# A two-layer sequence kernel: dt of each scan half made in a new order, deferred products over 60 of 64 steps

## The reference, cut to what matters

```python
xz = einsum('bsd,ed->bse', xn, in_proj_w); x_in, z = split(xz, 2, axis=-1)     # 1024 channels each
u = silu(causal_conv4(x_in) + conv_b)
dt_r, B, C = split(u @ x_proj_w.T, [64, 80], axis=-1)                          # 64, 16, 16 columns
dt = softplus(dt_r @ dt_proj_w.T + dt_proj_b);  A = -exp(A_log)                # A: 1024 x 16
h = h * exp(dt * A) + (dt * u) * B;  y = sum over the 16 states of h * C       # a scan over 1024 positions
y = (y + u * D) * silu(z);  x = x + gate * (y @ out_proj_w.T)
```

## Time and profile before

| | before |
|---|---|
| median of 3 runs (lowest, highest) | 7325.14 us (7324.45, 7329.71) |
| the profiled execution: time, span | 7318.66 us, 7317.1 us |
| PE busy | 6329.8 us (87%) |
| DVE busy | 5947.7 us (81%) |
| ACT busy | 4700.3 us (64%) |
| POOL busy | 3147.3 us (43%) |
| mean granted TensorE clock | 0.93 of 2.4 GHz |

### The profile page before, as it was taken

One profiled execution on the slowest core, in us unless ns is written; L12 is line 12 of the kernel. 1 busy time (PEld: TensorE's weight loads), 2 busy tenths in 40 slices (PEclk: granted clock), 3 DMA queues, 4 the chain that ended last, 5 costly groups with the idle time before them and its releaser, 6 DMA issues.

```text
span 7317.1 us, 135980 instructions
## 1 busy us (share of the span) xinstructions
PE 6329.8 (87%) x43360; PEld 4061.0 (55%) x43360; DVE 5947.7 (81%) x7137; ACT 4700.3 (64%) x6673; POOL 3147.3 (43%) x1533
## 2 busy tenths in 40 slices
PE   6998799987989879989799888898799987999878
PEld 2664457644575546745467445664457644575544
DVE  0678988789887998869978799778988799887995
ACT  2665677566675666746767467665677566675664
POOL 0105771067601774019730388105771067601773
PEclk9999899998999989999899998999899998999989
DMA  3425783367823777238752387425783367823676
GB/s 143 142 76 163 180 202 108 104 161 169 235 59 132 162 173 202 71 129 183 181 164 82 133 204 182 128 75 164 179 203 107 106 161 169 234 59 132 163 173 176
DMA packets 432975, 1092.28 MB, mean 149 GB/s; under 512 B 50056, under 2 KB 50184, under 8 KB 428000
## 3 DMA queue, kind: packets, MB, share of 16 engines
q1 hardware_dynamic: 256672, 671.49, 28.0%
q0 software_dynamic: 157120, 378.04, 26.6%
q10 hardware_dynamic: 18432, 33.56, 1.3%
HBM read 564.39 MB, written 250.10 MB: 111 GB/s over the span
## 4 chain that ended last, share of the span: by engine, by line
PE 70%; issue 10%; DVE 8%; DMA 4%; ACT 3%; POOL 3%; DVEq 1%; SPq 1%; ACTq 0%; POOLq 0%
PE ps L1233 43%; PE ps L1486 11%; PE ps L1334 9%; PE ps L1283 3%; POOL area_s L675 3%; DMA z_keep<-z_st 2%; DVE area_h L1156 2%; DVE area_s L1041 1%; PE ps L1285 1%; ACT k_stack L778 1%; DVE area_dt L1144 1%; PE ps L1435 1%; DMA k_stack<-qk_keep 1%; DMA area_acc<-area_w 1%; DVE area_u L1050 1%
## 5 line engine op out<-in xcount | busy, mean ns | idle before, releaser
L675 POOL TENSOR_TENSOR area_s<-area_u,area_s 128x1024 f32<-128x1024 f32 x1024 | 2537.0, 2547 | 667.3 <-DVE area_u L1147 385.0
L1156 DVE TENSOR_TENSOR_SCAN area_h<-ps,area_s 128x1024 f32<-128x1024 f32 x1024 | 2333.9, 2279 | 32.8 <-POOL area_s L675 19.1
L1486 PEld LDWEIGHTS ps<-ident,area_h 128*128 128x128 f32 x8192 | 1009.8, 151 | 960.8 <-DVE area_acc L1166 480.2
L1486 PE MATMUL ps<-ident,area_h 128*128 128x128 f32 x8192 | 1201.9, 294 | 383.3 <-DVE area_h L1156 205.7
L802 ACT ACTIVATE area_s<-area_s,negmax 128x1024 f32<-128x1024 f32 x1024 | 1177.3, 1150 | 519.8 <-DVE negmax L1041 517.4
L1041 DVE CUSTOM_DVE_ANT_0 area_s<-ps,area_dt 128x1024 f32<-128x1024 f32 x1024 | 1241.5, 1215 | 169.5 <-PE ps L1233 118.3
L662 POOL TENSOR_TENSOR area_s<-area_s 128x1024 f32<-128x1024 f32 x64 | 176.3, 2754 | 2651.8 <-ACT area_s L847 2651.8
L874 ACT ACTIVATE ps<-area_dt,negA 128x1024 f32<-128x1024 f32 x1024 | 1145.9, 1120 | 236.7 <-DVE area_h L1156 119.7
L860 ACT ACTIVATE area_w<-ps,C_nat 128x512 f32<-128x512 f32 x1024 | 704.4, 688 | 827.7 <-PE ps L1486 814.1
L1334 PE MATMUL ps<-ident,area_s 128*128 128x128 f32 x8192 | 1091.0, 277 | 16.6 <-ACT area_s L802 16.6
L1334 PEld LDWEIGHTS ps<-ident,area_s 128*128 128x128 f32 x8192 | 973.1, 143 | 168.7 <-issue 24.7
(11 more groups left out here) (125 smaller groups left out, 5598.8 us busy)
## 6 DMA issues: line engine op xcount, KB each, us to landing
area_acc<-area_w POOLq DMA_DIRECT2D x256, 1024.0 KB, 8.7
area_s<-b_rows SPq DMA_DIRECT2D x256, 512.0 KB, 5.1
q_stack<-qk_keep SPq DMA_DIRECT2D x520, 128.0 KB, 2.6
k_stack<-qk_keep SPq DMA_DIRECT2D x520, 128.0 KB, 3.2
qk_keep<-q_stack SPq DMA_DIRECT2D x144, 256.0 KB, 4.7
qk_keep<-k_stack SPq DMA_DIRECT2D x144, 256.0 KB, 5.2
area_s<-z_keep SPq DMA_DIRECT2D x72, 512.0 KB, 4.4
y_keep<-area_acc POOLq DMA_DIRECT2D x8, 4096.0 KB, 14.6
```

Of the source, the lines that this page charges most:

```text
L675: pool.tensor_tensor(dbu[:, dl % 2, :], U[:, k // (NS * DL) * DL + dl, :], bb[:, q, :], ALU.mult).then_inc(s_dbu.sem, 1)
L1156: v.tensor_tensor_scan(out=hs[:, q, dl, :], data0=banks(2 * (dl % 2)), data1=dbu[:, dl % 2, :], initial=0.0, op0=ALU.mult, op1=ALU.add).th ...
L1486: last = nc.tensor.transpose(ps[:, 4 + n % 2, dl * P:(dl + 1) * P], hs[:, r % 2, dl, n * P:(n + 1) * P], ident[:, :])
```

## The change

Line numbers here and in the rows that follow are those of the kernel before, where not said otherwise; in the listings of the changed order they are the changed kernel's.

- **Banks.** The dt products of tiles 0 to 3 go to banks 0, 2, 6 and 4 (`DT_BANK`), no more to 0, 2, 4, 6.
- **Order of dt.** On DVE clips, the pairs of L1144 and L1147, and scans alternate tile by tile; on ScalarE Exp and Ln of a tile follow one another (`soft`). At the second half PE makes the product of tile 4 behind the third scan of the last state, tile 5 ahead of that state's transposes, tile 6 within them and tile 7 after them, and DVE's and ScalarE's work on them stands between the last state's adds and scalings.
- **One table set.** Ahead of the copy of x_dbl ScalarE loads the set `natural_log_exp_and_others`, which has both functions.
- **Deferred products.** The 128 products are spread over the first 60 steps: product m stands in step m * 60 // 128. A row's flips stand behind its second and fourth `out` product.
- **Output adds** of GpSimd move with the units' steps: to steps 22, 37 and 52 from 23, 39 and 55.

```diff
+DT_BANK = (0, 2, 6, 4)
...
-ROW = 8
-FLIP_LAG, MOVE_LAG = 6, 6
+PRODUCTS, OVER, MOVE_LAG = 16 * NT, 60, 6
+def deferred_at(m):
+    return m * OVER // PRODUCTS
...
-        units.append(("z", j, 0, 7 - p, ROW * j + 1))
+        units.append(("z", j, 0, 7 - p, deferred_at(m + 3)))
...
-            units.append(("flip", j + 1, 0, 6 + p, ROW * j + 4))
-            units.append(("flip", j + 1, 1, 6 + p, ROW * j + 6))
-        units.append(("out", j, 0, 7 - p, ROW * j + 7))
+            units.append(("flip", j + 1, 0, 6 + p, deferred_at(m + 9)))
+            units.append(("flip", j + 1, 1, 6 + p, deferred_at(m + 11)))
+        units.append(("out", j, 0, 7 - p, deferred_at(m + 15)))
...
+                nc.scalar.preload_act_table_set("natural_log_exp_and_others")
                 act.wait_ge(*s_xd.at(b, 1))
...
+                soft(0)
+                soft(1)
+                decay_tile(0, 0, 0)
+                soft(2)
...
+                scale_by_c(0, NS - 2, NT - 1, 0)
+                for i in moves_at(NS * DL, NS * DL + 12):
+                    move_unit(i)
+                soft(4)
+                scale_by_c(0, NS - 1, 1, 1)
+                soft(5)
...
-                    clip(dg * DL + 2)
-                    clip(dg * DL + 3)
...
+                dt_and_dtu(0)
+                clip(2)
+                dt_and_dtu(1)
+                clip(3)
+                scan(0, 0, 0, 0)
...
-                    if s == 4 and j + 1 < NT:
-                        flip(j + 1, 0)
+                    if j + 1 < NT and k in (1, 3):
+                        flip(j + 1, k // 2)
...
+                        if r == NS - 1:
+                            pe.wait_ge(*s_h.at(b, r * DL + 3))
+                            project_dt(DL)
                         pe.wait_ge(*s_h.at(b, (r + 1) * DL))
+                        if r == NS - 1:
+                            project_dt(DL + 1)
...
-                            if r == NS - 1 and step in (1, 2):
-                                project_dt(DL + (step == 2))
+                            if r == NS - 1 and n == 3:
+                                pe.wait_ge(*s_ge.at(b, NU))
+                                project_dt(DL + 2)
+                        if r == NS - 1:
+                            pe.wait_ge(*s_acc.at(b, NS * DL))
+                            pe.wait_ge(*s_ev.at(b, NS * DL))
+                            project_dt(DL + 3)
```

More of the change, by code:

```diff
@@ new lines, in _ @@
+                soft(0)
+                soft(1)
+                decay_tile(0, 0, 0)
+                soft(2)
+                decay_tile(0, 0, 1)
+                soft(3)
+                decay_tile(0, 0, 2)
+                decay_tile(0, 0, 3)
+                for r in range(1, NS):
+                    decay(0, r)
+                scale_by_c(0, NS - 2, NT - 1, 0)
+                for i in moves_at(NS * DL, NS * DL + 12):
+                    move_unit(i)
+                soft(4)
+                scale_by_c(0, NS - 1, 1, 1)
@@ new lines, in _ @@
+                soft(5)
+                scale_by_c(0, NS - 1, 3, 1)
+                decay_tile(1, 0, 0)
+                scale_by_c(0, NS - 1, 5, 1)
+                scale_by_c(0, NS - 1, 7, 1)
+                decay_tile(1, 0, 1)
+                soft(6)
+                decay_tile(1, 0, 2)
+                soft(7)
+                decay_tile(1, 0, 3)
+                act.wait_ge(*s_zs.at(b, 16 * ZU))
+                act.nop(nofuse=True)
+                for r in range(1, NS):
+                    decay(1, r)
@@ L941, in _ @@
+                scale_by_c(1, NS - 2, NT - 1, 0)
+                for n in range(1, NT, 2):
+                    scale_by_c(1, NS - 1, n, 1)
+                    for _, i, low in copies_at(NS * DL + n // 2, NS * DL + 12 if n == NT - 1 else None):
+                        copy_unit(b + 1, i, low)
             for s in range(NT + 1):
@@ new lines, in _ @@
+                dt_and_dtu(0)
[3 more added lines that the diff above has]
+                scan(0, 0, 0, 0)
+                dt_and_dtu(2)
+                scan(0, 0, 0, 1)
+                dt_and_dtu(3)
+                scan(0, 0, 0, 2)
+                scan(0, 0, 0, 3)
+                with dve.Fori(0, NS // 2 - 1) as i:
+                    for q in (1, 0):
+                        for dl in range(DL):
+                            scan(0, i * 2 + (2 - q), q, dl)
+                            add(0, i * 2 + (1 - q), 2 * dl)
@@ new lines, in _ @@
+                for dl in range(DL):
+                    scan(0, NS - 1, 1, dl)
+                    add(0, NS - 2, 2 * dl)
+                clip(4)
+                clip(5)
+                add(0, NS - 1, 0)
+                add(0, NS - 1, 2)
+                dt_and_dtu(4)
+                add(0, NS - 1, 4)
+                dt_and_dtu(5)
+                add(0, NS - 1, 6)
+                clip(6)
+                scan(1, 0, 0, 0)
+                dt_and_dtu(6)
+                clip(7)
+                scan(1, 0, 0, 1)
@@ L1209, in _ @@
+                dt_and_dtu(7)
+                scan(1, 0, 0, 2)
+                scan(1, 0, 0, 3)
+                dve.wait_ge(*s_dul.at(b, 16))
+                for r in range(1, NS):
+                    for dl in range(DL):
+                        scan(1, r, r % 2, dl)
+                        add(1, r - 1, 2 * dl)
+                        next_norm(r * DL + dl)
+                for n in range(0, NT, 2):
+                    add(1, NS - 1, n)
             dve.wait_ge(*s_acc.at(B - 1, UN))
```

302 lines of the change are left out of this document (125 added, 177 removed).

## The result

The changed kernel takes **7388.58 us** (median; 7378.7 to 7395.76), the kernel before, measured beside it, 7324.8 us: ratio 1.0085, 95% interval 1.0067 to 1.0102. It is slower by 64 us where 18 us less was forecast.

A forecast was written before the change was run, and what follows sets the result against it. The prediction took DVE and PE as level and full in the first half, nothing near full at the seams. Per element -5.3 + 8.0 - 4.9 = -2.2, for eight -18, on the median 7325.1: 7307 us, range 7250 to 7347.

The forecast's parts named there:

- Seam 1: Opening of an element's first half, where dt is made: the new order on DVE gains 5.3 us per element.
- Table loads: ScalarE's table loads, nine fewer and one added per element: worth nothing, since they lie beside DVE's work.
- The second multiply: DVE's second multiply in the first seam: overlaps GpSimd's product by only 0.1 us, taken as 0 extra.
- Seam 2: Opening of the second half: starts right behind GpSimd's output add, then waits for du's load; gains 4.9 us per element.
- the free steps: The first half's last four steps, left without deferred products: DVE alone could begin the new half well before.
- The flips' waits: First half, before flips in even rows: PE waits for ScalarE to empty their PSUM bank, 5.4 us lost per element.
- Rival A: Waits at the flips don't count: the half costs 1 us instead of 8, 7251 us; chance 0.20.
- z's waits: First half: ScalarE's copies into z's one buffer come closer, waits for stores grow, 3.4 us per element landing on PE.
- PE's clock behind a stop: First half: half speed counted only at the opening, 3.0 us as before; nothing added behind PE's waits.
- Half: First half from PE's first step to its last: 178.1 us instead of 170.1, 8.0 us lost per element.
- Rival B: First half: z's late stores make all eight copy pairs wait, 12.2 us instead of 3.4, 7378 us; chance 0.12.

The follow-up runs named there:

- table_only: The kernel before with only the one table set loaded ahead of the copy of x_dbl, all orders as before: 7321.73 us, ratio 0.9998.
- over64: The changed kernel with deferred products over 64 steps again instead of 60, new order of both seams kept: 7253.87 us, ratio 0.9903.
- spread_only: The kernel before with only the deferred products spread over 60 steps, flips, copies and output adds moving along: 7415.84 us, ratio 1.0123.
- z_two: The changed kernel with two buffers for z's copies instead of one: 7286.96 us, ratio 0.9945.
- two_moves_first: The changed kernel with two buffers for z's copies and ScalarE's copies of deferred units ahead of its scaling: 7257.79 us, ratio 0.991.
- moves_first: The changed kernel with ScalarE's copies of deferred units ahead of its scaling in the same step: 7275.27 us, ratio 0.9932.
- parts_step0: The changed kernel with GpSimd's accumulating transfers of the parts issued one step earlier: 7405.4 us, ratio 1.0112.

## Why the prediction was wrong

The forecast was 7307, range 7250 to 7347; measured 7389. The chance of slower was 0.20.

- **Seam 1, 5.3 us per element: right.** First scan 651.12, 7.38 us after the last u·D product instead of 12.6; 7.3 was forecast. Over eight elements it gave 4.3 each, since the first element's old seam (12.63) was the longest; the others had 11.1 to 12.1. Taking one element eight times was 8 us too much.
- **Table loads, 0: right**, shown by table_only.
- **The second multiply, 0 extra: right.** It took 1.26 us, beside GpSimd's product of 646.57 to 648.93. The Trainium skill, "SBUF — State Buffer" (two separate sides), lets only their overlap count, 0.18 us as an estimate; the trace agrees in that the cost is no more than that: 0.03 us above the first multiply's 1.23.
- **Seam 2, 4.9 us: right in size**, 4.8 measured, and in its chain: GpSimd's product behind the output add, du's load last. I had du's 2 MB at 9.1 by its row; DVE's wait ended 10.6 after the issue. The Trainium skill, "DMA: Bandwidth & Descriptors" (Anatomy of one DMA), gave 6.8 as an estimate by its fit for GpSimd's transfers, and a gain of 5.3; the trace does not agree. But I put the gain down partly to the free steps. over64 shows that the order of dt alone gives it, spread_only that the free steps alone would have given it too; they don't add up.
- **The flips' waits, 5.4: right mechanism, measured 4.0** (z_two); the half gave back 2.5 of them when they were taken away (two_moves_first). Rival A is thereby out: PE has no room, its stops do count.
- **z's waits, 3.4: here it fell.** The step was "The two copies of a row are 2 x 2.84 = 5.68 apart now, 5.18 at PE's own pace, so each wait grows by 0.5". It let the copies move and kept the landing. The landing is not a property of the store: 6.7 us behind a part's transfer it is 5.4, 1.75 behind it 8.0 (row 4 in both kernels). The change moved 16 copies per element against transfers that stay on every fourth step, and the forecast never laid the two lists of steps side by side, though it did so for the output adds. The waits are 8.6 us per element (1.9 before), and the two buffers give back 11.9.
- **PE's clock behind a stop, 0: missed.** The sum counted a wait as its length. The opening's half speed stood in the same rows, and the low clock comes back behind a stop: 0.57 granted over 4 us behind row 4's, 1.5 us lost, 15 such stretches over the kernel.
- **Half, 8.0: measured 16.9**, the two steps above: 5.2 more of waits (8.6 for 3.4), some 3 of the low clock behind them, 1.4 less for flips; 2 stay unassigned.

Rival B named the right resource and side, and nearly the price (12.2 for 11.9, 7378 us for 7389), with the wrong distribution: not all eight pairs by 1.5, but four rows by up to 3.6. That its price fits is luck: 12.2 us were all waits, where 8.6 were waits and most of the rest was clock. Its reason, "output adds and accumulating transfers now fall into one step", holds for one of the three adds (step 37) and was the smaller part: in row 4 the output add is 0.7 of 3.5, over all rows 24 of 69 us. It had 0.12. What stood for it was in the trace before: row 2's second store landed after 2.4 us in the fourth element, 0.8 us behind a part's issue, and after 7.2 in the first, 1.85 behind. Setting the landings from 2.0 to 7.2 us beside the parts' issues would have shown the rule before the change.

## What to carry over

When a schedule is stretched, list everything that stays on its old steps, transfers first, and lay it beside what moves: a store's landing time belongs to its place behind the others, not to the store. Where two engines are level, a wait of the one that feeds them costs its full length and, behind the longer ones, the clock; a second buffer, the copy ahead of other work, or both turned a loss of 0.9% into a gain of 0.5 to 0.9%. And test the enabling part alone: the new order of dt needed no free steps, and the spreading gained time in no pairing that was run. It cost 135 us under the new seams as they stand and 92 under the old ones; with the copies first and two buffers both ways take the same (7257.8 and 7257.3).

## What the chip showed unexpectedly

- Landing of a 256 KB store from SBUF to HBM by its start behind the issue of a 1 MB accumulating transfer, means over eight elements of the changed kernel: 1.1 us behind 4.3 (row 0), 1.7 behind 8.1, 2.0 behind 6.9, about 10 or more behind, with no output add within 10 us, 2.1 to 2.5. Issued within 0.6 us of it, 2.0 to 3.3 (moves_first, parts_step0). It is worst a little behind, not beside it: the part's packets start 1.9 us behind its issue, and a store that comes after them stands behind them.
- The same store 2.0 us behind a 256 KB accumulating transfer lands in 2.0 us.
- The granted clock fell to its lower level for 3.4 us behind stops of PE of 2.1 to 4.2 us in a half otherwise full, though not behind each: never behind row 3's (2.0 to 2.2).
- 64 table loads less, 83 us of ScalarE, gave nothing within 0.1%: the page's most visible saving was worth least.
